# Softmax sums taken along with the transposed maxima, and sent back through DRAM instead of by four transposes a group

## What is computed

```python
def causal_attention(q, k, v):              # one sample, 16 heads, S = 512, DH = 32
    s = q @ k.T / sqrt(DH)                   # where key <= query, else masked
    p = exp(s - max(s, axis=-1))
    return (p @ v) / sum(p, axis=-1)         # then @ Wo + bo
```

## Time and profile before

| what | value |
|---|---|
| runs | 1732.76, 1733.81, 1736.29 us; median 1733.81 us |
| span of the profiled execution | 1732.7 us (its own run time is not listed apart from its span) |
| TensorE busy | 1657.8 us, 96% |
| VectorE busy | 1174.8 us, 68% |
| ScalarE busy | 977.3 us, 56% |
| GpSimd busy | 437.3 us, 25% |
| slots of the attention stage | about 300 to 1017 us |
| one sample (four slots) between 447 and 718 us | 90.3 us |

### The profile page before, as it was taken

One profiled execution on the slowest core, in us unless ns is written; L12 is line 12 of the kernel. 1 busy time (PEld: TensorE's weight loads), 2 busy tenths in 40 slices (PEclk: granted clock), 3 DMA queues, 4 the chain that ended last, 5 costly groups with the idle time before them and its releaser, 6 DMA issues.

```text
span 1732.7 us, 27454 instructions
## 1 busy us (share of the span) xinstructions
PE 1657.8 (96%) x9416; PEld 1331.5 (77%) x9416; DVE 1174.8 (68%) x2758; ACT 977.3 (56%) x2258; POOL 437.3 (25%) x670
## 2 busy tenths in 40 slices
PE   6799988899999999999999899999999999999999
PEld 4688766667676777767777568888999999999998
DVE  6799775777777767685867737767565656565643
ACT  5788753777676767676767654634242424242422
POOL 5788530323132313223231212010101010101010
PEclk8899998999999999999999989999999999999999
DMA  7122233443444434344433524576646464646451
GB/s 308 51 97 79 92 122 97 99 99 93 116 100 117 99 97 125 81 123 99 99 88 85 183 104 170 209 279 241 243 170 243 170 243 170 244 170 243 171 195 67
DMA packets 61826, 254.81 MB, mean 147 GB/s; under 512 B 10580, under 2 KB 15956, under 8 KB 45944
## 3 DMA queue, kind: packets, MB, share of 16 engines
q1 hardware_dynamic: 61688, 253.06, 44.8%
HBM read 153.93 MB, written 48.23 MB: 117 GB/s over the span
## 4 chain that ended last, share of the span: by engine, by line
PE 77%; DVE 9%; ACT 4%; DMA 4%; SPq 2%; issue 2%; POOL 1%; DVEq 0%; POOLq 0%; ACTq 0%
PE psum L82 21%; PE psum L83 20%; PE psum L84 20%; PE psum L1632 4%; PE psum L1660 3%; PE psum L1613 3%; SPq L920 2%; DVE psum L1165 2%; PE psum L1538 2%; ACT psum L1408 1%; DMA k_stack<-k_samples 1%; DMA k_raw<-in_w_in 1%; DVE k_tokens L1216 1%; DVE k_samples L1206 1%; PE psum L1556 1%
## 5 line engine op out<-in xcount | busy, mean ns | idle before, releaser
L1408 ACT ACTIVATE psum<-psum,b_mx 128x512 f32<-128x512 f32 (+3 forms) x512 | 259.1, 507 | 199.4 <-DVE b_mx L1165 197.2
L1165 DVE CUSTOM_DVE_ANT_0 psum<-psum,b_mask 128x512 f32<-128x512 f32 (+3 forms) x512 | 244.4, 504 | 141.8 <-PE psum L1613 141.0
L2489 ACT ACTIVATE k_act<-k_stack_f,k_smalls 128x512 f32<-128x512 f32 x112 | 81.0, 723 | 336.5 <-DVE k_stack_f L2277 336.5
L1418 ACT ACTIVATE k_exps<-psum 128x512 f32<-128x512 f32 (+1 forms) x384 | 204.1, 533 | 20.6 <-PE psum L1632 18.7
L1632 PE MATMUL psum<-k_stack 98*128 98x512 f32 (+3 forms) x512 | 159.3, 353 | 16.5 <-ACT k_exps L1418 16.2
L2130 POOL TENSOR_SCALAR k_result<-k_result,k_pb 128x512 f32<-128x512 f32 x32 | 59.9, 1886 | 448.4 <-DVE k_result L2196 448.4
L2256 DVE TENSOR_TENSOR k_act_lo<-k_act,k_act_hi 128x512 fp32r<-128x512 f32 x112 | 77.3, 691 | 130.9 <-ACT k_act_hi L2492 130.8
L1613 PE MATMUL psum<-k_stack 96*128 96x512 f32 (+3 forms) x512 | 150.1, 335 | 2.5 <-ACT psum L1408 2.5
L82 PE MATMUL psum<-k_act_hi,k_w_hi 128*128 128x512 f32 x384 | 150.9, 393 | 0.6 <-DVE k_act_lo L2256 0.6
L83 PE MATMUL psum<-k_act_lo,k_w_hi 128*128 128x512 f32 x384 | 150.7, 392 | 0.0
L84 PE MATMUL psum<-k_act_hi,k_w_lo 128*128 128x512 f32 x384 | 150.4, 392 | 0.0
(11 more groups left out here) (368 smaller groups left out, 4563.7 us busy)
## 6 DMA issues: line engine op xcount, KB each, us to landing
k_stack<-w_factors SPq DMA_DIRECT2D x35, 1792.0 KB, 8.0
k_stack<-k_samples SPq DMA_DIRECT2D x384, 128.0 KB, 2.4
k_weights<-w_factors SPq DMA_DIRECT2D x17, 1792.0 KB, 7.6
x<-k_tokens SPq DMA_DIRECT2D x10, 1024.0 KB, 4.1
k_tokens<-x SPq DMA_DIRECT2D x8, 1024.0 KB, 5.0
d<-k_result SPq DMA_DIRECT2D x32, 256.0 KB, 2.5
k_raw<-x SPq DMA_DIRECT2D x8, 1024.0 KB, 4.8
k_raw<-d SPq DMA_DIRECT2D x8, 1024.0 KB, 7.0
```

What stands on the lines that cost most here:

```text
L1165: last = dve.tensor_tensor_reduce(got, got, mask[:, S - width:S], -INV_SQRT_DH, -2.0 * MASKED, ALU.add, ALU.min, mx[n % 2][:, h, t:t + 1])
L1408: act.activation(sc(n, u)[:, at:at + width], sc(n, u)[:, at:at + width], ACT.Exp, bias=mx[n % 2][:, h, t:t + 1], scale=-1.0, accum_out=sum ...
L1418: act.activation(exps[n % 2][:, h, at:at + width], by_key(n, u)[:, 0:width], ACT.Exp, scale=INV_SQRT_DH).then_inc(k_act, 1)
L2489: act.activation(act_f[:], whole_tile, ACT.Gelu, bias=small(smalls, "b1", 2 * pair % M + second)).then_inc(pair_gelu, 1)
```

## The change

The sums of group n - 1 are now written into the same tile as the maxima of group n (`cols`, with the maxima in columns 0 to 7 and 48 to 55, and the sums in columns 32 to 47). The transpose of the first maxima, at step 8, takes 48 columns instead of 8, and so brings the 16 sums of the group before to partitions 32 to 47 of bank 1. The reciprocal is taken there, on 16 partitions by 128 columns. One DMA writes the result to a small DRAM tensor, a second reads it back with each head's row repeated for 32 partitions, into the tile `over`. `spread_recs` and `recs_back` are gone, and with them the name "bc" in the ring of two banks. The last group has a transpose of its own (`last_sums`). The rename of `x_ld` to `sample_ld` in the feed-forward part frees a semaphore and counts the same loads.

```diff
-    bc = [("bc", *divmod(n - 2, G), "dve")] if 0 <= n - 2 < GROUPS else []
...
     if g == 2:
-        return qk + each("tb", b + 1, range(J), "act") + bc + each("wo", b - 1, range(J - 1), "dve")
+        return qk + each("tb", b + 1, range(J), "act") + each("wo", b - 1, range(J - 1), "dve")
...
-    mx = [sb(f"mx{k}", [P, HG, T]) for k in range(2)]
+    cols = [sb(f"cols{k}", [P, SUMS_AT + HG * T + 2 * T]) for k in range(2)]
...
+    sum_at = lambda n, h, t: cols[(n + 1) % 2][:, SUMS_AT + T * h + t:SUMS_AT + T * h + t + 1]
+    rec_rows = keep["maxima"][REC_ROWS:REC_ROWS + HG * T, :].bitcast(F32)
...
+        def recs_out(n):
+            sp.wait_ge(rec_set, n + 1)
+            if n:
+                sp.wait_ge(rec_moved, 32 * n)
+            sp.dma_start(io["recs"].rearrange("h (t q) -> (h t) q", t=T), rec_rows).then_inc(rec_moved, 16)
+
+        def recs_in(n):
+            sp.wait_ge(rec_moved, 32 * n + 16)
+            if n:
+                sp.wait_ge(over_set, n)
+            sp.dma_start(over[:], io["recs"].unsqueeze(1).to_broadcast([HG, DH, S])).then_inc(rec_moved, 16)
...
                 if 0 <= n < GROUPS:
                     max_rows(n, 0)
+                if 0 <= n - 1 < GROUPS:
+                    recs_out(n - 1)
...
                 if 0 <= n + 1 < GROUPS:
                     stack_rows(n + 1, (2, 3))
+                if 0 <= n - 1 < GROUPS:
+                    recs_in(n - 1)
...
-        def spread_recs(n):
-
-            pool.wait_ge(rec_set, n + 1)
-            if n:
-                wait_full(pool, ("bc", *divmod(n - 1, G)))
-            pool.tensor_copy(rec_rows, recs[:].rearrange("p h t -> p t h").unsqueeze(3).to_broadcast([P, T, HG, DH])).then_inc(rec_spread, 1)
...
         def invert(n):
-            dve.wait_ge(e_act, exps_until(n, UNITS - 1))
+            dve.wait_ge(max_full, 2 * n + 3)
             if n:
-                dve.wait_ge(rec_spread, n)
-            dve.reciprocal(recs[:], sums[n % 2][:]).then_inc(rec_set, 1)
+                dve.wait_ge(rec_moved, 32 * n - 16)
+            dve.reciprocal(rec_rows, sums_out(n)).then_inc(rec_set, 1)
 
         def over_sums(n):
-            name = ("bc", *divmod(n, G))
-            wait_full(dve, name)
+            dve.wait_ge(rec_moved, 32 * (n + 1))
             dve.wait_ge(ctx_out, n + 1)
-            dve.tensor_tensor(ctx_at(n), ctx_at(n), pj(name), ALU.mult).then_inc(pj_dve, 1)
+            dve.tensor_tensor(ctx_at(n), ctx_at(n), over[:], ALU.mult).then_inc(over_set, 1)
...
             if u == 1 and 0 <= n - 1 < GROUPS:
                 maxima_out(n - 1, 1)
-                invert(n - 1)
+                if n == GROUPS:
+                    invert(n - 1)
             if u == 8 and 0 <= n < GROUPS:
                 maxima_out(n, 0)
+                if n:
+                    invert(n - 1)
...
+            if half:
+                pe.transpose(max_out, mx_at(n, 2, 0, 2 * T), ident[:]).then_inc(max_full, 1)
+            else:
+                if n:
+                    pe.wait_ge(e_act, exps_until(n - 1, UNITS - 1))
+                pe.transpose(ctx_bank[0:SUMS_AT + HG * T, 0:P], cols[n % 2][:, 0:SUMS_AT + HG * T], ident[:]).then_inc(max_full, 1)
...
-        def recs_back(n):
-
-            pe.wait_ge(rec_spread, n + 1)
-            out = claim(("bc", *divmod(n, G)))
-            for t in range(T):
-                last = pe.transpose(out[:, t * P:(t + 1) * P], rec_rows[:, t, :, :].rearrange("p h d -> p (h d)"), ident[:])
-            last.then_inc(pj_full, 1)
...
-            if u == 7 and 0 <= n - 2 < GROUPS:
-                recs_back(n - 2)
```

More of the change, by code:

```diff
@@ L727 @@
 AFTER = B
+SUMS_AT, REC_ROWS = 32, 64
 U_TILES = ((T - 1,), (T - 2, 0), (1,))
@@ L771, in bank_uses @@
     if g == 0:
-        return qk + each("st", b + 1, range(J), "dve") + bc + v + after_back
+        return qk + each("st", b + 1, range(J), "dve") + v + after_back
     if g == 1:
-        return qk + each("tin", b + 1, range(T), "act") + bc + v
+        return qk + each("tin", b + 1, range(T), "act") + v
     if g == 2:
-        return qk + each("tb", b + 1, range(J), "act") + bc + each("wo", b - 1, range(J - 1), "dve")
-    return qk + each("wo", b - 1, (J - 1,), "dve") + after_in + v[:2 * (n < 0)] + bc + each("p", b + 2, (0,), "dve") + v[2 * (n < 0):]
+        return qk + each("tb", b + 1, range(J), "act") + each("wo", b - 1, range(J - 1), "dve")
+    return qk + each("wo", b - 1, (J - 1,), "dve") + after_in + v[:2 * (n < 0)] + each("p", b + 2, (0,), "dve") + v[2 * (n < 0):]
 PJ, PJ_TAKEN, _taken = {}, [], {"act": 0, "dve": 0}
@@ L811, in attention_engines @@
     d_out, v_other = keep["result"][:, 0::2, :], keep["result"][:, 1::2, :]
-    rec_rows = keep["early"][:].rearrange("p (t h d) -> p t h d", t=T, h=HG)
+    over = keep["early"]
     xh, xl = keep["normed"][:, 0:J, :], keep["normed"][:, J:2 * J, :]
@@ L830, in attention_engines @@
     gate_h = sb("gate_h", [P, B])
-    strength, mod, half_b2 = sb("strength", [P, B]), sb("mod", [P, B]), sb("half_b2", [P, 1])
+    strength, mod, half_b2 = (cols[0][:, at:at + w] for at, w in ((2 * T, B), (2 * T + B, B), (2 * T + 2 * B, 1)))
     halves = (slice(0, B // 2), slice(B // 2, B))
@@ L872, in attention_engines @@
     max_out = ctx_bank[0:2 * T, 0:P]
+    sums_out = lambda n: ctx_bank[SUMS_AT:SUMS_AT + HG * T, 0:P] if n < GROUPS - 1 else ctx_bank[SUMS_AT:SUMS_AT + HG * T, P:2 * P]
     def wait_full(eng, name):
```

34 lines of the change are left out of this document (22 added, 12 removed).

## The result

The changed kernel takes 1743.08 us (median of 4 runs, 1741.84 to 1746.43), the kernel before 1733.87 us beside it (4 runs, 1732.76 to 1736.29). The ratio is 1.0055, 95% interval 1.0039 to 1.0071: slower by 9.2 us. The prediction was 1734 us, 1726 to 1742 us; it put the likeliest case at no change and gave slower 0.33. Run again at another time, the changed kernel gave 1.0066 (1.0045 to 1.0088).

What follows compares the result with a forecast made beforehand. TensorE, 96% busy, was taken as the bound, waiting in places on ScalarE behind VectorE. Shed transposes -9.8 us and the longer reciprocal +9.6 us gave -0.2 us, so 1734 us, range 1726 to 1742 us.

Steps and rivals of the forecast that it cites:

- the likeliest case: The whole kernel: no change within about 0.2%, 1730.5 to 1737.5 us, chance 0.41.
- three signs of being wrong: Reciprocal below 0.6 or above 1.1 us; L1258 waiting for the load; the sample's period moving by over 0.5 us.
- What PE sheds: Attention stage: TensorE's gain from the removed transposes, 9.8 us in all, nothing in the first two of a sample's four slots.
- g = 2: 1.19 us: Third slot of a sample: 0.67 us from L82 starting earlier, 0.36 us bank wait gone, 0.16 us refill; 1.19 us gained.
- L1245's successor reads SBUF where it read PSUM, same shape: nothing: The division on VectorE: reading its operand from SBUF instead of PSUM costs nothing.
- g = 3: 0.15 us: Fourth slot of a sample: the transpose of the maxima moves 0.15 us earlier, limited by ScalarE's copy L1446.
- I take 0.86 us: Reciprocal of 16 x 128 in step 8: 0.86 us, losing 0.86 and 0.65 us in a sample's first two slots.
- Samples 0 and 7: 1.8 us gained, 0.5 lost: Samples without the full pattern: small gains from fewer transposes, some 0.5 us lost to the reciprocal in sample 7.
- The way through DRAM hidden: Store and load of the reciprocals: needed a whole slot later, so landing in time and costing nothing.
- rival 3: DMA queue: the store delays the six stack DMAs that VectorE's L1177 awaits; 11 us slower, 1745 us; chance 0.11.
- The transposes of 48 columns: Transpose of the maxima, 48 wide instead of 8: costs nothing, at most a quarter of 0.44 us, 3.4 us in all.
- Rival 2: Reciprocal longer than forecast: slower, 1.3 us per 0.1 us; 1738 us at 1.2 us, 1749 us at 2.0 us; chance 0.22.

Runs made afterwards that it cites:

- e1: The kernel before with one of the four spread transposes of L1670 made, three quarters of the spread quotients left out: 1729.88 us, ratio 0.9973.
- e5: The changed kernel with a plain copy for GpSimd's subtract L1022, low parts of the split left out: 1741.9 us, ratio 1.0048 to the kernel before.
- e6: The changed kernel with a plain copy in place of the step 8 reciprocal, quotients left out: 1731.71 us, ratio 0.9983 to the kernel before.
- e10: The changed kernel with the reciprocal over 64 of 128 columns from the second group on: 1734.17 us, ratio 0.9993 to the kernel before.
- e11: The changed kernel unaltered, run again at another time: 1746.68 us, ratio 1.0066 to the kernel before.
- e4: The kernel before with the division's second operand from an SBUF tile by a maximum, instead of a PSUM bank, division left out: 1736.41 us, ratio 1.0016.
- e3: The changed kernel with the reciprocal on 128 x 16 in step 1 before the transpose, a copy in step 8: 1730.19 us, ratio 0.9975 to the kernel before.
- e8: The changed kernel with reciprocal and division one step later on VectorE, behind the maximum of unit 9: 1729.18 us, ratio 0.9977 to the kernel before.

## Why the prediction was wrong

The mechanism was in the main the one predicted (PE sheds transposes in g = 2, VectorE's longer chain costs g = 0 and g = 1); the sizes were not, and two terms left at nothing were not nothing: the operand in SBUF, and the later start of the wide transpose. Of the three signs of being wrong that the prediction names, one came: the sample's period moved by 1.46 us. (Its "g = 0 22.0 us" is a slip; the slot was 20.80 us.)

- **"What PE sheds", g = 0 and g = 1: nothing.** Right. L1667 waits for ACT's L1462 in g = 1 (0.49 us), and e1's regular samples gain nothing in these two slots.
- **g = 2: 1.19 us.** Right in itself and lost again. L82 starts 1.54 us ahead of its slot's context_out (603.32) where it was 0.87 us ahead (601.46), the 0.67 us of the prediction. Where the division is done in time (e5, e6, e10) the slot is 1.14 to 1.17 us shorter; in the changed kernel 0.61. The step that failed is "L1245's successor reads SBUF where it read PSUM, same shape: nothing". It costs 0.55 us a sample, some 3.4 us.
- **g = 3: 0.15 us.** Wrong: +0.07. L1646 stood 0.20 us behind the end of L1446. In e1 it stands 0.14 us behind, and the slot is 0.09 us shorter, so something was there to gain; but L1667 never starts less than 0.25 us behind the copy. 6 x 0.22 = 1.3 us.
- **"I take 0.86 us."** The main miss. It is 0.95 us, and what counts on the chain is 1.10: 0.04 us of gap and 0.11 us of hand-over come with it. The line went through two rows with different partitions and sources; the third point at 128 columns puts 6.25 ns where I had 5.4. g = 0 lost 0.99 for 0.86, and g = 1 lost 1.01 for 0.65. The slack of 0.21 us in g = 1 was right: against its slot's context_out, step 11's matmul comes 5.82 us behind where it came 4.91, 0.91 us later. The term left out is the 0.10 us by which the next matmul follows later once PE has stood (0.23 for 0.13 us, rows of g = 1); the prediction had such a refill for g = 2 alone. e6, with 0.28 us of copy and the same 0.15 beside it, fits: 0.43 - 0.21 + 0.10 = 0.32, measured 0.33. Together 0.5 us a sample, 3.0 us.
- **Samples 0 and 7: 1.8 us gained, 0.5 lost.** Wrong in sign. From one context_out to the fourth after it, the first stretch of the stage takes 90.77 us (before: 88.27), the seventh 87.35 (84.03); with a copy for the reciprocal (e6) they take 88.30 and 83.94. So in these traces the reciprocal costs the two stretches 2.5 and 3.4 us, and I had priced only the full pattern. These are single executions, and the sizes are not firm: the seventh stretch of the changed kernel is 86.16 us in e11, and that of e4, whose regular sample is within 0.2 us of the kernel before, is 85.68. The second stretch, 93.04 against 90.30, belongs here too: in e6 it is 92.07, in e3 90.51. How much of it is the reciprocal is open.
- **The way through DRAM hidden: nothing.** Right. L1258 never waits for the load, SP's queue has the same waits, and rival 3 is refuted.
- **The transposes of 48 columns: nothing.** Wrong by 0.11 us. L1667 takes 0.27 us as L1646 did, but starts 0.25 to 0.26 us behind ACT's copy where 0.14 us was the shortest in the kernel before; so it is in every kernel that has it. Its weight load takes 0.10 us for 0.08 us; it also has one more wait, for ACT's exponentials, behind the wait for the copy. No run parts the two. In g = 1 the later wait in step 11 takes it up, in g = 3 it is most of the difference between e1 and the changed kernel.

The sum of the misses: 3.4 + 1.3 + 3.0 = 7.7 us for the regular samples. Through the whole stage, from the first context_out to the last, the two traces differ by 694.7 - 682.3 = 12.4 us where the prediction had -0.2, so some 5 us more of the miss come from both ends and the second stretch, less what the two long samples of the kernel before take off. The rest of the program, which the change doesn't touch, took 4.7 us less in that execution; the other traces vary there by as much, so the timed +9.2 and +10.9 us are the better measure.

Rival 2 (the reciprocal is longer) names the direction, but its law of 1.3 us for each 0.1 us gives 1735 us for 0.95. The price measured between e6 and the changed kernel is 11.4 us for 0.67, or 1.7 us for each 0.1. It is not even: e10 has paid only a small part of it at 0.55 us, and the collision and the ends come with the rest.
## What to carry to other kernels

Before an operation is priced, list what is queued behind it on its engine and follow that list to the engine that bounds the kernel; put a long operation behind whatever the bounding engine waits for, and not before it (e8: the same instructions one step later, 14 us). When work per element is turned from 128 partitions x 16 into 16 partitions x 128, its time on VectorE grows with the columns (0.25 to 0.95 us), so do it ahead of the transpose (e3). When an operand moves from PSUM to SBUF, look at what GpSimd does at that moment. And when an instruction gets one more wait or a wider operand, look at how far behind its releaser it starts, not only at its duration.
